# A graph network kernel: reciprocals of small tiles in the attention merge, own features and x loaded a stage early, the edge layer's last step in the third norm

## The reference

```python
h = jnp.maximum(_layernorm(x, axis=-1), 0.0)
x = x + _L0_gnn_ref(h, ...)             # three rounds of mean over neighbours, matmul, relu
h = jnp.maximum(_layernorm(x, axis=-1), 0.0)
x = x + _L1_gnn_ref(h, ...)             # attention, 4 heads of 32
h = jnp.maximum(_layernorm(x, axis=-1), 0.0)
x = x + _L2_gnn_ref(h, ...)             # edge layer
h = jnp.maximum(_layernorm(x, axis=-1), 0.0)
x = x + _L3_gnn_ref(h, edge_attr)       # sum of neighbours and edge features

# attention: every node is also its own neighbour
alpha = jnp.exp(alpha - amax[dst]); denom = segment_sum(alpha, dst)
out = segment_sum(xh[src] * (alpha / denom[dst])[:, :, None], dst)
h = out + gat_b + h
return h + gelu(layer_norm(h, ln2_g, ln2_b) @ w1 + b1) @ w2 + b2

# edge layer
z = (1.0 + eps) * h + aggr
z = relu(batchnorm(z @ W1, g1, b1))
z = relu(batchnorm(z @ W2, g2, b2))
return z + h
```

## Time and profile before

| | us |
|---|---|
| runs | 13256.12, 13263.81, 13250.01 (median 13256.12) |
| the profiled execution's own time | 13269.17 |
| its span, first to last instruction | 13267.2 |
| busy: GpSimd / TensorE / VectorE / ScalarE | 9013.3 / 6021.2 / 3452.2 / 1221.1 |
| mean granted TensorE clock | 0.589 of full speed |

### The profile page before, as it was taken

How to read it: one execution, slowest core, us unless ns; L and a number is a source line. 1 busy time by engine, 2 the same in 40 slices (tenths; PEclk the granted TensorE clock), 3 DMA queues, 4 the chain that set the end, 5 groups by cost and what they waited for, 6 DMA issues and landing times. The chain is left out here.

```text
span 13267.2 us, 102459 instructions
## 1 busy us (share of the span) xinstructions
PE 6021.2 (45%) x27058; PEld 4761.4 (36%) x27059; DVE 3452.2 (26%) x6432; ACT 1221.1 (9%) x2429; POOL 9013.3 (68%) x9490
## 2 busy tenths in 40 slices
PE   3444444344444444444354444665444546333333
PEld 2433333333333333333344333433333333333333
DVE  4222222111111222222344444452222225111111
ACT  1000000000000000000011000042222222000000
POOL 1777776777777677777577777217777760777776
PEclk9555555555555555555566666587666678555555
DMA  3222222222222222222333333223333332222222
GB/s 101 55 55 55 55 55 51 54 55 55 55 56 55 59 67 67 67 68 70 72 86 86 84 84 84 67 98 102 105 102 102 102 95 103 61 61 61 61 61 58
DMA packets 519276, 956.93 MB, mean 72 GB/s; under 512 B 173853, under 2 KB 328106, under 8 KB 517588
## 3 DMA queue, kind: packets, MB, share of 16 engines
q0 software_dynamic: 301056, 623.59, 18.6%
q1 hardware_dynamic: 218112, 332.26, 8.1%
HBM read 847.12 MB, written 108.07 MB: 72 GB/s over the span
## 5 line engine op out<-in xcount | busy, mean ns | idle before, releaser
L744 POOL DMA_INDIRECT work<-rows_a,index x4704 | 4468.3, 950 | 1595.7 <-issue 1550.6
L772 PE MATMUL psum<-onehot,work 128*128 128x80 f32 x12544 | 2713.2, 413 | 4079.1 <-DMA work<-rows_a,index 2948.1
L772 PEld LDWEIGHTS psum<-onehot,work 128*128 128x128 f32 x12544 | 2628.4, 322 | 4166.4 <-issue 4165.5
L1496 POOL DMA_INDIRECT regionC<-attention_rows,index x1568 | 1526.6, 974 | 548.3 <-issue 477.6
L913 POOL DMA_INDIRECT work<-rows_b,index x1568 | 1491.6, 951 | 567.4 <-issue 518.7
L744 POOL DMA_INDIRECT work<-rows_b,index x1568 | 1480.7, 944 | 540.6 <-issue 518.1
L996 PE MATMUL psum<-regionB,onehot 128*80 128x256 f32 x3136 | 939.1, 473 | 1022.3 <-ACT regionB L973 1022.3
L831 DVE TENSOR_TENSOR regionA<-regionA,psum 128x80 f32 x784 | 185.3, 236 | 4523.3 <-PE psum L772 4314.0
L996 PEld LDWEIGHTS psum<-regionB,onehot 128*80 128x80 f32 x3136 | 589.1, 192 | 1344.6 <-issue 1222.0
L184 POOL COPY work<-regionB 128x500 f32 (+1 forms) x75 | 45.3, 603 | 977.7 <-DVE regionB L653 977.7
L1060 DVE TENSOR_TENSOR regionB<-work,psum 128x512 f32<-128x512 f32 x392 | 243.1, 682 | 1528.8 <-DMA work<-rows_b,index 1528.8
(11 more groups left out here) (347 smaller groups left out, 6956.3 us busy)
## 6 DMA issues: line engine op xcount, KB each, us to landing
regionB<-in_edge_attr SPq DMA_DIRECT2D x195, 512.0 KB
work<-rows_a,index POOLq DMA_INDIRECT x4704, 2.5
work<-rows_b,index POOLq DMA_INDIRECT x3136, 2.5
work<-edge_columns SPq DMA_DIRECT2D x98, 512.0 KB
regionC<-attention_rows,index POOLq DMA_INDIRECT x1568
x_transposed<-regionA SPq DMA_DIRECT2D x75, 250.0 KB, 6.3
rows_a<-regionC SPq DMA_DIRECT2D x50, 250.0 KB
regionB<-h_transposed SPq DMA_DIRECT2D x2, 5250.0 KB, 17.0
```

The lines of the kernel that those rows point to most:

```text
L744: pool.indirect_dma_start(rows3[h][:, t, :], None, table, bass.IndirectOffsetOnAxis(ap=net.index[:, k, h * ST + t:h * ST + t + 1], axis=0) ...
L772: last = nc.tensor.matmul(bank_of(h, q, 0), rows3[h][:, t, :], onehot[:, h * ST + t, :], start=(k == 0), stop=(k == GT - 1))
L1496: pool.indirect_dma_start(ring[s][:, t, :], None, net.XH, bass.IndirectOffsetOnAxis(ap=net.index[:, k, t:t + 1], axis=0)).then_inc(gathere ...
```

## The change

In the merge the turns are gone. `den` starts at `TINY` in place of 0. For each chunk TensorE makes, straight from `den` (8 rows), four totals of 125 columns on four groups of 32 partitions (`pick`) and the own weights on 128 partitions (`own_pick`); VectorE subtracts `TINY` and takes the reciprocal of a tile of 128 x 125; TensorE spreads it with four matmuls, as the norms do. The own features are loaded into `B` in this stage, chunk by chunk, once `den` of the chunk has been read. `gat_output` then loads x into `A` for n2, chunk by chunk, behind `up`. `gin_output` loads x into `C` after `C` has been stored, and leaves its last two steps to n3: there ScalarE does the relu (`last`, lag 0) and VectorE's `add_x` is two additions.

```diff
@@ normalise
-            if not first:
-                sp.dma_start(A[:, 0:LEAD * CH], net.XT[:, 0:LEAD * CH]).then_inc(s["loaded"], 16)
-                sp.dma_start(A[:, LEAD * CH:N], net.XT[:, LEAD * CH:N]).then_inc(s["rest"], 16)
...
             def add_x(c, k):
-                if isinstance(c, int) and c == LEAD:
-                    dve.wait_ge(s["rest"], 16)
-                nc.vector.tensor_tensor(net.col(A, c), net.col(A, c), net.col(B, c),
+                if pending:
+                    dve.wait_ge(s["last"], c + 1)
+                    nc.vector.tensor_tensor(net.col(A, c), net.col(A, c), net.col(B, c),
+                                            ALU.add).then_inc(s["part"], 1)
+                    dve.wait_ge(s["part"], c + 1)
+                nc.vector.tensor_tensor(net.col(A, c), net.col(A, c), net.col(Cc if pending else B, c),
                                         ALU.add).then_inc(s["x_ready"], 1)
...
+            def last(c, k):
+                nc.scalar.activation(net.col(A, c), net.col(A, c), ACT.Relu,
+                                     bias=pending[0], scale=pending[1]).then_inc(s["last"], 1)
@@ gat_pass
-            V.memset(B[32:64, :], 0.0)
+            V.memset(B[32:64, :], TINY)
@@ gat_merge, new body
+            sp.dma_start(Cc[:, 0:LEAD * CH], net.XHT[:, 0:LEAD * CH]).then_inc(s["xh"], 16)
+            sp.dma_start(Cc[:, LEAD * CH:N], net.XHT[:, LEAD * CH:N]).then_inc(s["rest"], 16)
+            with sp.Fori(0, NCH) as c:
+                sp.wait_ge(s["total"], c + 1)
+                sp.sem_inc(s["carried"], 1)
+                sp.dma_start(net.col(B, c), net.HT[:, bass.ds(c * CH, CH)]).then_inc(s["h"], 16)
...
+            def total(c, k):
+                if c > 1:
+                    pe.wait_ge(s["small"], c - 1)
+                    pe.wait_ge(s["merged"], c - 1)
                 for j in range(4):
+                    T.matmul(net.psum[32 * j:32 * j + 32, k * 512:k * 512 + SUB], pick,
+                             den[:, c * CH + j * SUB:c * CH + (j + 1) * SUB], start=True, stop=True)
+                T.matmul(bank(4 + k), own_pick, den[:, c * CH:(c + 1) * CH], start=True, stop=True
+                         ).then_inc(s["total"], 1)
+            def spread(c, k):
+                pe.wait_ge(s["inverse"], c + 1)
+                for j in range(4):
+                    x = T.matmul(net.psum[:, (2 + k) * 512 + j * SUB:(2 + k) * 512 + (j + 1) * SUB],
+                                 selectors(net)[:, j * P:(j + 1) * P], small[k], start=True, stop=True)
                 x.then_inc(s["spread"], 1)
             for c in range(NCH + 1):
                 if c < NCH:
+                    total(c, c % 2)
                 if c:
+                    spread(c - 1, (c - 1) % 2)
...
+            dve.wait_ge(s["xh"], 16)
+            def invert(c, k):
+                dve.wait_ge(s["total"], c + 1)
+                if c > 1:
+                    dve.wait_ge(s["spread"], c - 1)
+                V.tensor_scalar(small[k], bank(k, SUB), -TINY, None, ALU.add).then_inc(s["small"], 1)
+                dve.wait_ge(s["small"], c + 1)
+                V.reciprocal(small[k], small[k]).then_inc(s["inverse"], 1)
             def merge(c, k):
+                if c == LEAD:
+                    dve.wait_ge(s["rest"], 16)
+                dve.wait_ge(s["total"], c + 1)
+                V.tensor_tensor(net.col(Cc, c), net.col(Cc, c), bank(4 + k), ALU.mult).then_inc(s["step"], 1)
+                dve.wait_ge(s["step"], c * 2 + 1)
+                V.tensor_tensor(net.col(A, c), net.col(A, c), net.col(Cc, c), ALU.add).then_inc(s["step"], 1)
+                dve.wait_ge(s["step"], c * 2 + 2)
+                dve.wait_ge(s["spread"], c + 1)
+                V.tensor_tensor(net.col(A, c), net.col(A, c), bank(2 + k), ALU.mult).then_inc(s["merged"], 1)
+            for c in range(NCH + 1):
+                if c < NCH:
+                    invert(c, c % 2)
+                if c:
+                    merge(c - 1, (c - 1) % 2)
@@ gat_output
-            sp.dma_start(B[:, 0:LEAD * CH], net.HT[:, 0:LEAD * CH]).then_inc(s["h"], 16)
...
-            sp.dma_start(B[:, LEAD * CH:N], net.HT[:, LEAD * CH:N]).then_inc(s["rest"], 16)
+            with sp.Fori(0, NCH) as c:
+                sp.wait_ge(s["up"], c + 1)
+                sp.sem_inc(s["carried"], 1)
+                sp.dma_start(net.col(A, c), net.XT[:, bass.ds(c * CH, CH)]).then_inc(s["x"], 16)
+            sp.wait_ge(s["x"], 16 * NCH)
@@ gin_output
             sp.wait_ge(s["kept"], 16)
+            sp.dma_start(Cc[:, 0:N], net.XT).then_inc(s["x"], 16)
+            sp.wait_ge(s["x"], 16)
...
-            with dve.Fori(0, NCH) as c:
-                dve.wait_ge(s["last"], c + 1)
-                nc.vector.tensor_tensor(net.col(B, c), net.col(A, c), net.col(B, c),
-                                        ALU.add).then_inc(s["sum"], 1)
+            dve.wait_ge(s["step"], 16)
...
-            with act.Fori(0, NCH) as c:
-                nc.scalar.activation(net.col(A, c), net.col(A, c), ACT.Relu,
-                                     bias=shift[:, 2:3], scale=scale[:, 2:3]).then_inc(s["last"], 1)
```

More of the change, by code:

```diff
@@ L574, in normalise @@
     s = {k: net.sem(f"{tag}_{k}") for k in
[L575 removed]
+         ("last", "part", "x_brought", "x_turned", "x_ready", "brought", "mean", "centred", "squared", "var", "dev",
           "inverse", "selectors", "spread", "h", "turned", "rows", "saved", "stored", "kept", "carried")}
@@ L1863, in gat_merge @@
     A, B, Cc, V = net.A, net.B, net.C, net.nc.vector
[L1864 to L1872, removed]
+    s = {k: net.sem(f"gm_{k}") for k in ("xh", "rest", "ready", "total", "small", "inverse", "spread", "merged",
+                                         "step", "carried", "h")}
+    den = B[32:32 + 2 * H, :]
+    pick, own_pick = net.wtmp[32:32 + 2 * H, 0:32], net.wtmp[32:32 + 2 * H, P:2 * P]
+    ident8 = net.ident[32:32 + 2 * H, 32:32 + 2 * H]
+    small = [net.work[:, k * 512:k * 512 + SUB] for k in range(2)]
+    bank = lambda k, n=CH: net.psum[:, k * 512:k * 512 + n]
     with nc.Block() as block:
@@ L1882, in _ @@
             T = nc.tensor
[L1883 to L1897, removed]
-                for j in range(4):
-                    x = T.transpose(net.psum[0:2 * H, (2 + k) * 512 + j * SUB:(2 + k) * 512 + (j + 1) * SUB],
-                                    both[:, (c * 4 + j) * 2 * H:(c * 4 + j + 1) * 2 * H], net.ident[0:SUB, 0:SUB])
-                x.then_inc(s["back"], 1)
@@ L1927, in _ @@
         @block.vector
         def _(dve):
-            count = [0]
-            def done(ins):
-                count[0] += 1
-                ins.then_inc(s["step"], 1)
-                dve.wait_ge(s["step"], count[0])
-            V.memset(shifted, 0.0).then_inc(s["shift"], 1)
-            dve.wait_ge(s["shift"], 1)
-            V.tensor_copy(shifted[:, H:2 * H], net.ident[0:H, 0:H]).then_inc(s["shift"], 1)
-            dve.wait_ge(s["wide"], 1)
-            for k in range(2):
-                x = V.tensor_copy(select[k], net.psum[0:2 * H, 1024 + k * P:1024 + (k + 1) * P])
@@ L1978, in gat_output @@
     s = {k: net.sem(f"go_{k}") for k in
-         ("weights", "h", "rest", "gat_b", "selectors", "spread", "inverse", "sum", "mean", "centred", "squared", "var", "dev",
+         ("weights", "x", "gat_b", "selectors", "spread", "inverse", "sum", "mean", "centred", "squared", "var", "dev",
           "carried", "scaled", "normed", "up", "gelu", "down", "out")}
@@ L2102, in gin_output @@
     s = {k: net.sem(f"gi_{k}") for k in
-         ("weights", "up_weights", "eps", "h", "rest", "step", "z", "first", "stat", "deviation", "up", "hid", "down", "out", "last",
-          "sum", "kept")}
+         ("weights", "up_weights", "eps", "h", "rest", "step", "z", "first", "stat", "deviation", "up", "hid", "down", "out", "x", "kept")}
     def fold(dve, k, gain, bias, wait, count):
```

61 lines of the change are left out of this document (15 added, 46 removed).

## The result

The changed kernel took 13234.03 us (median of 18 runs, 13221.42 to 13242.82), the kernel before, on the same occasion, 13262.24 us (18 runs, 13250.01 to 13279.44). The ratio is 0.9977, 95% interval 0.997 to 0.9984: some 28 us less, and at least 21. The profiled execution took 13226.45 us, with a span of 13224.9.

The account below looks back on a forecast made before the run. Gather stages fill nearly all the span, unchanged; in five short stages between, whatever ends each sets its time. 8.5 - 4.7 - 4.4 - 18.5 + 3.4 = -15.7 us, so 13240.4 from a median of 13256.12; range 13214 to 13262.

Parts of the forecast that it names:

- n3's term of +3.4: Third norm: 2.4 us less at the start, 4.5 more to the first row store, 1.3 more for the first few stores.
- Merge, +8.5 forecast: Merge: work ahead of the loop goes, but VectorE idles 2.7 us per turn behind `total`; turn 6.1 us, 8.5 us more.
- gat_output, -4.7 forecast: Start of gat_output: VectorE no longer waits for h, 3.5 us, and a second wait goes, 1.2; 4.7 us less.
- n2, -4.4 forecast: Second norm: VectorE starts at 8776.03 in place of 8780.48, and the stores start earlier by the same; 4.4 us less.
- Edge layer's output, -18.5 forecast: End of that stage: relu and addition go, 18.3 us, with a little more; the new x load costs nothing; 18.5 us less.
- the prediction's own sign of being wrong: Third norm: the prediction called itself wrong if VectorE and not the stores ends the stage.
- A second size: Third norm, ahead of the first row store: each of some six turns grows by an addition of 0.72; 4.5 us more.
- Base: Whole kernel: the forecast was carried to a median of 13256.12 us for the kernel before, giving 13240.4.
- The clock did not rise in the changed merge: Merge rival: TensorE at 2.4 GHz, turn 5.0 us, -41 in all, 13215; chance 0.10.
- The picks ran side by side: Merge rival: the four picks run one behind the other, 1.27 us more per turn, +13 in all, 13269; chance 0.07.
- n3's clock rose: Third norm rival: TensorE stays at the low clock, turn about 5.3 us, +21 in all, 13277; chance 0.05.
- The gather stages moved: Stages that gather rows: none changes; the prediction is wrong if one moves by more than a few us.

Follow-up runs that it names:

- e4: Kernel before, with x for n3 loaded a stage early into C, relu and addition staying where they were; 0.9999 of the kernel before.
- e7: Changed kernel, `total` waiting only for the first step of the merge two chunks back, picks and own weights with 128 rows; 13179.79 us, 0.9939.
- e11: Kernel before, with the merge's wide matmuls given 128 rows in place of 8, the added rows zero; 13218.27 us, 0.9962.
- e5: Changed kernel, `total` waiting only for the first step of the merge two chunks back, `spread` for the whole merge; 13206.41 us, 0.9956.
- e1 to e4: Kernel before with one part each: new merge, 0.9997; x for n2 loaded early, 0.9995; relu and addition in n3, 0.9988; x for n3 loaded early, 0.9999.

## Why the prediction was right or wrong

The forecast of -15.7 was in the right direction and the measured time lies inside the range, but n3's term of +3.4 was not borne out, and the change gave 12 us more than forecast.

- **Merge, +8.5 forecast, +5.3 measured.** The mechanism was right: order, idle (2.7 forecast, 2.78 measured), clock 0.50. The sizes were off by small sums: XHT's first piece let VectorE start 4.7 us into the stage, not 5.9; a turn is 6.00, not 6.1, 2.3 over 23 turns, since the steps overlap at their ends (the reciprocal takes 0.94, and the next step starts 0.85 behind its start); the last merge 2.0 in place of 2.2. Against it 0.5 us more from the last step to the next stage.
- **gat_output, -4.7 forecast, -5.6 by the means.** First step 2.15 us into the stage, before 5.89: 3.7, taken as 3.5. The rest, the second wait and what came behind it, gave 1.9 to 3.0 in place of 1.2.
- **n2, -4.4 forecast, -8.8 in the two first traces, -4.7 by the means.** The start gave 4.4 as read. The other half of the -8.8 was the scatter of the stores (4.05 and 3.89 us in these two traces, up to 4.43 in others).
- **Edge layer's output, -18.5 forecast, -17.6 by the means**, right; the added load of x stuck out nowhere.
- **n3, +3.4 forecast, -6.8 in the two first traces, -2.1 by the means: the step that failed.** "I take the pace of n3's own rows", 3.77 us. It was one execution's. The same code ran at 3.38 to 3.77 in five traces (3.65 in e4, which has no load there), and n0's rows, cited as the lower bound (3.46), were the better evidence that such a pace moves. The changed form has 3.37 to 3.48 in six traces, level with VectorE's new turn (3.44, forecast 3.4). So the prediction's own sign of being wrong, VectorE and not the stores ending n3, came half true: VectorE sets the pace, and the last store goes 5.8 us behind ScalarE's last copy. How much n3 gains is not known to the microsecond: without the first trace, before's form has a mean of 117.2 us against 116.5, well inside the scatter, so what is shown is that the +3.4 is absent. A second size was off: each turn's longer work was to delay the first row store by 4.5 us; that store comes 25.53 us into the stage (before 25.91), which leaves 2.1 for it.
- **Base.** The median of the three runs shown was 13256.12; of 18 it is 13262.24. The measured 13234.03 is 6 below the forecast of 13240.4, but the difference of -28 is 12 more than the forecast of -15.7; the base hid half of the error. That is luck: the three runs shown happened to lie 6 us under the median of 18.
- **The rivals.** The clock did not rise in the changed merge. The prediction chose 0.50 by two stretches, one of matmuls with few rows and one of 128 rows busy 6.60 of 9 us; that few rows were the cause is what e7 and e11 then showed. The picks ran side by side. n3's clock rose (0.98 in its loop). The gather stages moved by about 6 us in all between the two executions.

## What to carry to other kernels

Where a stage's end hangs on how fast stores drain, one trace gives a sample and not a constant: take the same code's pace in several places or executions before an edit beside it is costed. A matmul that uses few rows of the array is worth a look at the granted clock beside it; filling the rows with zeros cost two memsets here and gave back 56 us of a stage of 146 (the whole kernel: 41 us by the medians). And a wait between engines should name the step that frees the buffer, not the last step of the group: one such wait was worth 33 us. A mean DMA share near one half does not show that DMA has room: count the packets of a store, and look at how many partitions it has.

## What was not expected of the hardware

- In e5 TensorE was at a granted clock of 0.50 (1.2 GHz) through 104.00 busy us of 104; each turn has picks and own weights of 8 rows, 2.7 us of it, and then `spread` with 128. In e7, where the same picks and own weights had 128 rows, 120 of them with weights of zero, it was at 1.00 (2.4 GHz), busy 53.30 of 78. These matmuls cost the same with 8 rows and with 128 at the same clock (picks 0.64 and 0.65, own weights 2.03 and 2.04).
- The pace of one and the same sequence of stores varies by a tenth between executions of the same kernel (n0 3.10 to 3.65 us per chunk, n3 of before's form 3.38 to 3.77), while the merge, bound by engines, repeats to 0.1 us.
- On one occasion the kernel before took 15433 us in place of 13262. The traces of e1 to e4, from that occasion, have all of it in the stages that gather (the edge pass 2475 to 2479 us for 2036 to 2047 in the other traces, the last stage 2270 to 2274 for 2014 to 2017); before's merge took 145.7 us both times. Why was not looked into.
- Moving the row stores to a second queue gave nothing in n2, though the 16 DMA engines were only 0.57 busy by the mean; ScalarE, which then issued them, stood for 4.85 us in one issue. A row store of 125 partitions carries 5 packets of 4 bytes and a store of 128 partitions 16, and on 5 engines the row stores and the others together would fill them (106%).
